# A selective-scan layer in one block: the scan starts after the first chunk's softplus, the other chunks' softplus moves into the scan's units

## The chip, the cores and the metric

The kernel runs on one core of a Trainium2 chip. Its five engines run at the same time, each with a queue of its own, and wait for one another through semaphores: TensorE (PE, matrix products), VectorE (DVE), ScalarE (ACT, activation functions from tables), GpSimd (POOL) and SyncE (SP, which here only issues DMAs). The metric is the time of one execution on the device in microseconds (us), the median of several runs; lower is better.

## The reference

Eight layers follow one another on a residual stream `x` of 2048 tokens by 128 features. The change touches only the first, a selective state-space layer (Mamba) with a feed-forward layer behind it. Cut to what matters:

```
x  = layer_norm(x)                       # twice: the outer norm, then the layer's own
xz = x @ in_proj_w;  xi, z = split(xz)   # 256 channels each
xc = silu(causal_conv4(xi) + conv_b)
dt, B, C = split(xc @ x_proj_w)          # 8, 16, 16 columns
dt = softplus(dt @ dt_proj_w + dt_proj_b)
A  = -exp(A_log)                         # 256 channels x 16 states
for each token t:                        # a recurrence over all 2048
    h = exp(dt[t] * A) * h + dt[t] * B[t] * xc[t]
    y[t] = sum over the 16 states of h * C[t]
y  = (y + D * xc) * silu(z)
x  = x + y @ out_proj_w
x  = x + gelu(layer_norm(x) @ ffn_w1 + ffn_b1) @ ffn_w2 + ffn_b2
```

## The kernel before

Channels lie on the 128 partitions, in two halves (H = 2), and tokens on the free axis, in C = 4 chunks of 512 columns (CW). The layer is made of two blocks. Between two blocks all engines meet at a barrier.

The first block is the projection. For each chunk TensorE transposes the normalised input (`turn`), multiplies it with convolution taps (`taps`) and with the gate weights (`gate`), computes B, C and the rank-8 part of dt (`b_c_rank`), and from the latter the raw dt (`steps_dt`). ACT evaluates the products: `take_taps` and `take_gate` with Silu, `take_high` copies B and C to bf16. Since B and C are wanted to full precision, they are kept as three bf16 parts: `take_high`, then DVE's `first_rest`, ACT's `take_middle`, DVE's `last_rest`, ACT's `take_low`. The softplus is computed as max(v, 0) + ln(1 + exp(-|v|)): ACT's `take_abs` (L561) writes |v| into `dtx`, DVE's `relu_dt` (L404) writes max(v, 0) into `dt`, ACT then runs Exp over two chunks at a time (`exp_of`, L567) and Ln over chunk 0 and chunks 1 to 3 (`ln_of`, L572). At its end DVE adds the two for chunk 0 (L449) and multiplies with `xc` (L451). DVE's `outer_norm` (L379) makes `xo`, the base of the residual, and POOL's `add_bias` (L321) adds a bias to X.

The second block is the scan. It has U = 64 units, one for each chunk and state, chunk by chunk. In unit u TensorE spreads one row of B over all partitions and one of C (`spread`, L632 and L636), DVE multiplies `dtx` with B (`dBx`, L773), ACT computes the decays exp(dt * A) of both halves into PSUM (L720), DVE runs the recurrence of each half (`tensor_tensor_scan`, L784), ACT copies the last column of an earlier unit's `h` (`keep_state`, L712) and C (`Cs`, L726), POOL multiplies h with C (`hC`, L855), and TensorE adds it up over the states (`y_sum`, L645). Everything is double-buffered by u % 2. At the start of each later chunk DVE finishes the one before: `skip` (L756), `gated` (L761), then TensorE's `project` (L654) and DVE's `residual` (L766), which stands in DVE's queue in the fourth unit ahead of its scans. In units 0 to 11 POOL also adds the two parts of the softplus for chunks 1 to 3 (L845) and multiplies with `xc` (L849). SP's `fill` (L100) writes blank rows to memory for the next layer. Behind the last unit follows the feed-forward layer, in the same block.

Each engine's queue is written out in program order, so an instruction that waits holds up all behind it.

Of the kernel before, what the change touches and what calls it, by code (L numbers as in the profile page):

```python
# [24 lines left out]
U32 = mybir.dt.uint32  # L25
ALU = mybir.AluOpType
# [6 lines left out]
P = 128  # L33
# [151 lines left out]
def mamba(k):  # L185
# [22 lines left out]
    with tmp:  # L208
# [47 lines left out]
        s_dtm, s_abs, s_rel, s_exp, s_ln, s_A, s_dt, s_dtx, s_xb = (  # L256
            k.sem("m_" + n) for n in ("dt_mm", "dt_abs", "dt_relu", "dt_exp", "dt_ln", "A", "dt", "dtx", "x_plus_b"))
        col = lambda n: t[n].rearrange("(p o) -> p o", o=1)
        blocks = lambda n: t[n].rearrange("(h p) -> p h", p=P)

        with nc.Block() as block:
            @block.sync
            def _(sp):
                def x_chunk(c):
                    sp.dma_start(k.X[:, tiles_of(c), :],
                                 t["x"][c * CW:(c + 1) * CW, :].rearrange("(t p) d -> p t d", p=P)).then_inc(x_in[c], 16)

                with nc.allow_non_contiguous_dma(reason="small weights"):
                    x_chunk(0)
                    sp.dma_start(cwr[:], t["conv_wT"].rearrange("(o k) d -> o (k d)", o=1)).then_inc(w_in, 16)  # L270
                    sp.dma_start(inw[:], t["in_proj_w"]).then_inc(w_in, 16)
                    sp.dma_start(g1[:], col("ln1_g")).then_inc(w_in, 16)
                    sp.dma_start(b1[:], col("ln1_b")).then_inc(w_in, 16)
                    for c in range(1, C):
                        x_chunk(c)
                    for dst, src in ((cb[:], blocks("conv_b")), (xpw[:], t["x_proj_w"].rearrange("(h p) k -> p h k", p=P)),
                                     (dtw[:], t["dt_proj_w"]), (dtb[:], blocks("dt_proj_b")),
                                     (A[:], t["A_log"].rearrange("(h p) n -> p h n", p=P)),
                                     (w2b[:], t["ffn_b2"].partition_broadcast(P))):
                        sp.dma_start(dst, src).then_inc(w_xp, 16)  # L280
                    for dst, src in ((Dp[:], blocks("D")), (outw[:], t["out_proj_w"].rearrange("(h p) d -> p h d", p=P)),
                                     (g2[:], col("ln2_g")), (b2[:], col("ln2_b")), (w1[:], t["ffn_w1"]),
                                     (w1b[:], t["ffn_b1"].rearrange("(f p) -> p f", p=P)),
                                     (w2[:], t["ffn_w2"].rearrange("(f p) d -> p f d", p=P))):
                        sp.dma_start(dst, src).then_inc(w_out, 16)
                sp.wait_ge(w_out, 16 * 7)

            @block.gpsimd
            def _(pool):
                g = nc.gpsimd  # L290
                exact = dict(allow_small_or_imprecise_dtypes=True)
                g.memset(k.ident[:], 0.0)
                g.memset(k.ones[:], 1.0)
                g.memset(k.mhalf[:], -0.5).then_inc(c_zero, 1)
                pool.wait_ge(c_zero, 1)
                g.affine_select(out=k.ident[:], in_=k.ident[:], compare_op=ALU.not_equal, fill=1.0, base=0,
                                pattern=[[-1, P]], channel_multiplier=1).then_inc(c_id, 1)
                for n, part in enumerate((slice(0, CT), slice(CT, T))):
                    pool.wait_ge(s_ve, n + 1)
                    g.tensor_tensor(both[:, part], both[:, part], k.mhalf[:, part], ALU.pow).then_inc(s_rs, 1)  # L300
                g.memset(xp4[:], 0.0).then_inc(m_z, 1)
                pool.wait_ge(w_xp, 16 * 6)
                pool.wait_ge(m_z, 1)
                g.tensor_copy(xp4[:, :, 0, 0:R], xpw[:, :, 0:R])
                for part in range(1, 4):
                    last = g.tensor_copy(xp4[:, :, part, :], xpw[:, :, R:R + BC])
                last.then_inc(m_xp, 1)
                pool.wait_ge(s_ve, 3)
                g.tensor_tensor(k.rstd[:], k.veps[:], k.mhalf[:, 0:T], ALU.pow).then_inc(s_rs, 1)
                g.memset(sel[:], 0.0).then_inc(m_z, 1)  # L310
                pool.wait_ge(m_z, 2)

                def select(part):
                    g.affine_select(out=sel[:], in_=sel[:], compare_op=ALU.not_equal, fill=1.0, base=-32 * part,
                                    pattern=[[-1, BC], [0, P]], channel_multiplier=1).then_inc(m_sel, 1)
                    pool.wait_ge(m_sel, part)

                def add_bias(c):
                    pool.wait_ge(s_xo, c + 1)
                    xt = k.X[:, tiles_of(c), :]  # L320
                    g.tensor_tensor(xt, xt, w2b[:, None, :].to_broadcast([P, CT, P]), ALU.add).then_inc(s_xb, 1)  # L321

                select(1)
                select(2)
                select(3)
                g.memset(state[:], 0.0)
                g.memset(k.blank[:], 0.0)
                g.memset(k.onesb[:], 1.0)
                g.memset(k.tri[:], 1.0).then_inc(c_more, 1)
                add_bias(0)  # L330
                g.iota(k.each[:], pattern=[[1, k.E]], base=0, channel_multiplier=0, **exact)
                g.iota(k.first_row[:], pattern=[[k.REGION, k.E]], base=0, channel_multiplier=0, **exact)
                g.iota(k.step[:], pattern=[[1, k.step.shape[1]]], base=0, channel_multiplier=0, **exact)
                g.iota(k.token[:], pattern=[[k.N, 2], [P, T]], base=0, channel_multiplier=1)
                pool.wait_ge(c_more, 1)
                g.affine_select(out=k.tri[:], in_=k.tri[:], compare_op=ALU.is_gt, fill=0.0, base=0, pattern=[[1, P]],
                                channel_multiplier=-1)
                g.iota(k.blank[:, :, P].bitcast(U32), pattern=[[P, 2 * k.E]], base=2 * k.N, channel_multiplier=1)\
                    .then_inc(k.made_blank, 1)
                add_bias(1)  # L340
                add_bias(2)
                add_bias(3)

            @block.vector
            def _(dve):
                v = nc.vector

                def stats(c):
                    dve.wait_ge(x_in[c], 16)
                    for i in range(c * CT, (c + 1) * CT):  # L350
                        last = v.bn_stats(k.stats[:, i, :], k.X[:, i, :])
                    last.then_inc(s_st, 1)
                    dve.wait_ge(s_st, c + 1)
                    for i in range(c * CT, (c + 1) * CT):
                        last = v.bn_aggr(k.meanvar[:, i, :], k.stats[:, i, :])
# [2346 lines left out]
```

## Time and profile before

| | |
|---|---|
| median of 3 runs | 1608.6 us (1608.26 to 1610.08) |
| the profiled execution's own time | 1608.58 us |
| its span, first to last instruction | 1606.5 us |
| mean granted TensorE clock | 0.871 |
| busy share of the span | PE 75%, DVE 55%, ACT 40%, POOL 33% |
| the first layer | about the first 368 us |
| end of TensorE's projection work, first dBx | 64.4 us, 80.34 us |

Times of a timeline are from the span's start. Idle time of an engine is printed with what ended it. The granted clock is a share of 2.4 GHz. A row that reads "x2" holds two instructions back to back, which overlap a little.

### The profile page before, as it was taken

The numbers are of one execution on the slowest core, as the hardware profiler recorded it, in microseconds if no ns is written. First come the engines' busy times: TensorE is split into PE (matmuls) and PEld (weight loads), VectorE is DVE, ScalarE is ACT, GpSimd is POOL, SyncE is SP. The second block draws the span as 40 slices with busy tenths as digits, with TensorE's granted clock in tenths as the row PEclk, the third lists the DMA queues.
The fourth block names the chain that finished last, engine by engine and source line by source line (L and its number), as shares of the span: only waits on it lengthen the run. The fifth ranks groups of instructions, "written<-read, shape, count | busy, mean of one in ns | idle before, by whom it ended". The sixth has DMA issues, their size and how long they took to land. (4 is left out here: it accounts for less than half of the span.)

```text
span 1606.5 us, 23917 instructions
## 1 busy us (share of the span) xinstructions
PE 1209.1 (75%) x8263; PEld 726.7 (45%) x8271; DVE 878.5 (55%) x2054; ACT 649.7 (40%) x1106; POOL 531.0 (33%) x661
## 2 busy tenths in 40 slices
PE   8676766784389665089944999969954899969997
PEld 3222222244267444056622777734322676744544
DVE  3498999965244444133346888853662666741110
ACT  2664545541012101033313777637633666632221
POOL 6086656521723210712235222120026444200000
PEclk9789999996589865589975999979975999979999
DMA  2099400004121204111120000010000000020000
GB/s 53 0 197 188 67 1 1 0 1 159 52 54 52 78 6 157 52 44 42 34 79 1 2 2 2 2 41 1 1 9 0 2 2 2 2 75 0 0 0 27
DMA packets 87883, 59.76 MB, mean 37 GB/s; under 512 B 15331, under 2 KB 78709, under 8 KB 87638
## 3 DMA queue, kind: packets, MB, share of 16 engines
q1 hardware_dynamic: 83222, 48.86, 14.2%
q0 software_dynamic: 4544, 9.38, 1.8%
q8 instruction: 69, 1.13, 0.3%
q14 instruction: 48, 0.39, 0.1%
HBM read 29.69 MB, written 28.52 MB: 36 GB/s over the span
## 5 line engine op out<-in xcount | busy, mean ns | idle before, releaser
L855 POOL TENSOR_TENSOR hC<-h,Cs 128x1024 f32<-128x1024 f32 x64 | 153.2, 2394 | 86.8 <-DVE h L784 85.2
L645 PE MATMUL bank<-hC,ident 128*128 128x512 f32 x256 | 135.4, 654 | 41.3 <-POOL hC L855 41.3
L784 DVE TENSOR_TENSOR_SCAN h<-bank,state,dBx 128x512 f32<-128x512 f32 x128 | 157.3, 1271 | 2.2 <-ACT bank L720 0.2
L1157 POOL DMA_INDIRECT moe_answers<-moe_yw,moe_xg x78 | 74.7, 958 | 174.7 <-DVE moe_yw L1254 174.7
L2103 DVE TENSOR_REDUCE window_mx<-bank 128x2 f32<-128x384 f32 x128 | 69.6, 556 | 75.8 <-PE bank L1958 74.8
L1221 ACT ACTIVATE moe_hT<-bank 128x512 f32<-128x512 f32 x78 | 46.6, 597 | 155.5 <-PE bank L1184 155.5
L2103 DVE TENSOR_REDUCE decay_mx<-bank 128x2 f32<-128x512 f32 x128 | 85.2, 686 | 23.8 <-PE bank L1958 23.5
L720 ACT ACTIVATE bank<-dt,A 128x512 f32<-128x512 f32 x128 | 83.2, 682 | 36.5 <-DVE h L784 36.4
L2073 ACT ACTIVATE decay_pb<-bank 128x512 f32<-128x512 f32 x128 | 75.6, 597 | 47.8 <-PE bank L1971 45.1
L645 PEld LDWEIGHTS bank<-hC,ident 128*128 128x128 f32 x256 | 46.4, 200 | 106.1 <-POOL hC L855 68.2
L1193 PE MATMUL bank<-moe_wd,moe_hT 128*128 x624 | 84.5, 280 | 1.9 <-DVE moe_yw L1254 1.9
L178 ACT ACTIVATE xnT<-bank 128x512 f32<-128x512 f32 x24 | 14.3, 597 | 176.6 <-PE bank L169 176.6
L1167 PE MATMUL bank<-ident,moe_xg 128*128 128x128 f32 x78 | 22.5, 289 | 83.1 <-DMA moe_xg<-moe_slots 75.0
L1174 PE MATMUL bank<-moe_wa,moe_xgT 128*128 x156 | 83.4, 617 | 0.0
L967 POOL DMA_INDIRECT moe_slots<-moe_rows,moe_slot x64 | 61.6, 963 | 59.8 <-DVE moe_slot L1060 40.9
L158 POOL TENSOR_TENSOR rstd<-veps,mhalf 128x4 f32<-128x4 f32 (+1 forms) x14 | 23.3, 1662 | 171.3 <-DVE veps L140 171.1
L1193 PEld LDWEIGHTS bank<-moe_wd,moe_hT 128*128 128x128 f32 x624 | 77.5, 196 | 2.6 <-issue 2.6
L2073 ACT ACTIVATE window_pb<-bank 128x384 f32<-128x384 f32 x128 | 61.5, 486 | 40.1 <-PE bank L1971 39.8
L773 DVE TENSOR_TENSOR dBx<-dtx,bank 128x1024 f32<-128x1024 f32 x64 | 76.6, 1197 | 0.9 <-remote 0.9
L726 ACT ACTIVATE Cs<-bank 128x512 f32<-128x512 f32 x64 | 38.2, 596 | 78.9 <-POOL hC L855 58.1
L169 PE MATMUL bank<-ident,xn 128*128 128x128 f32 x64 | 17.2, 424 | 68.5 <-DVE xn L149 68.4
L2604 DVE TENSOR_TENSOR f_ys<-bank,f_s 128x512 f32<-128x512 f32 x4 | 2.8, 692 | 119.4 <-PE bank L2563 119.4
(455 smaller groups left out, 2933.4 us busy)
## 6 DMA issues: line engine op xcount, KB each, us to landing
moe_slots<-blank SPq DMA_DIRECT2D x16, 1040.0 KB, 17.9
moe_xg<-moe_slots SPq DMA_DIRECT2D x78, 65.0 KB, 1.8
moe_wa<-in_moe_w SPq DMA_DIRECT2D x2, 2048.0 KB
moe_back<-moe_answers SPq DMA_DIRECT2D x16, 256.0 KB, 4.7
moe_ba<-in_moe_b SPq DMA_DIRECT2D x1, 2048.0 KB
moe_wu<-in_moe_wu SPq DMA_DIRECT2D x1, 2048.0 KB
deep_w<-in_deep_w SPq DMA_DIRECT2D x3, 512.0 KB, 5.1
moe_answers<-moe_yw,moe_xg POOLq DMA_INDIRECT x78, 2.2
```

What stands on the lines that cost most here:

```text
L645: last = nc.tensor.matmul(sum_bank(hh)[:], k.ident[:], hC[:, u % 2, hh, :], start=(n == 0), stop=(n == NS - 1))
L720: nc.scalar.activation(decay_bank(u, hh)[:], dt[:, hh, cols(c)], ACT.Exp, scale=A[:, hh, n:n + 1]).then_inc(q_dA, 1)
L773: v.tensor_tensor(dBx[:, u % 2], dtx[:, :, cols(c)], b_bank[:, None, :].to_broadcast([P, H, CW]), ALU.mult).then_inc(q_dBx, 1)
L784: v.tensor_tensor_scan(h[:, u % 2, hh, :], decay_bank(u, hh)[:], dBx[:, u % 2, hh, :], state[:, n, hh:hh + 1], ALU.mult, ALU.add).then_inc ...
L855: g.tensor_tensor(hC[:, u % 2], h[:, u % 2], Cs[:, u % 2, None, :].to_broadcast([P, H, CW]), ALU.mult).then_inc(q_hC, 1)
L967: nc.gpsimd.indirect_dma_start(slots, bass.IndirectOffsetOnAxis(index, 0), rows[j][:, i, :], None)\
L1157: nc.gpsimd.indirect_dma_start(answers, bass.IndirectOffsetOnAxis(index, 0), yw[:, i % NY, :], None)\
L1174: nc.tensor.matmul(bank[1 + i % 2][:], xgT[:, i % 2, :], flat(wa), start=True, stop=True).then_inc(s_g, 1)
L1193: last = nc.tensor.matmul(bank[6][:, 0:P], hT[:, i % 2, f, :], wd[:, one, f, :].rearrange("p o d -> p (o d)"), start=(f == 0), stop=(f == ...
L1221: nc.scalar.activation(hT[:, i % 2].rearrange("p f q -> p (f q)"), bank[5 + 2 * (i % 2)][:], ACT.Copy if gated else ACT.Relu).then_inc(s_h ...
L2073: nc.scalar.activation(pb[:, w % 4, :], bank[2 + w % 2][:, 0:2 * HW], ACT.Exp).then_inc(s_ex, 1)
L2103: nc.vector.tensor_reduce(mx[:, 2 * g:2 * g + 2], bank[g % 2][:, 0:2 * HW].rearrange("p (j q) -> p j q", j=2), AX.X, ALU.max, negate=True) ...
```

## The change

Both blocks' queues go into one block, so no barrier stands between them; each engine runs its projection queue and then its scan queue. In detail:

- `take_abs` and `relu_dt` go. ACT's `take_rates` copies the raw dt from PSUM to `dt` with the bias (Identity, two per chunk). `size_of` (Abs), `positive_of` (Relu), `exp_of` and `ln_of` then work on one chunk of 1024 columns each from SBUF.
- ACT loads one named table set for Exp and Ln ahead of them. Before the scan it runs `exp_of` and `ln_of` for chunk 0 only, then `take_high`(2), `take_low`(1), `take_high`(3), `take_rates`(2), `take_rates`(3).
- Chunk 0's sum is one DVE instruction, max(dt, 0) + dtx; chunks 1 to 3 get their Relu on ACT.
- ACT's scan units 1 to 12 hold the other chunks' Abs, Relu, Exp and Ln, one each; units 13, 14 `take_middle`(2), (3) and units 18, 19 `take_low`(2), (3). DVE's units 15, 16 hold `last_rest`(2), (3).
- POOL's sums and products for chunks 1 to 3 stand in units 5 to 16; the outer norm of chunks 2 and 3 moves from DVE to POOL, units 18 and 22, with `add_bias` in units 20 and 24.
- SP issues the fill at once, without a barrier before it.

```
 project_scalar, end
+            for hh in range(H):
+                act.wait_ge(s_dtm, H * c + hh + 1)
+                nc.scalar.activation(dt[:, hh, cols(c)], dt_bank(c, hh)[:], ACT.Identity, bias=dtb[:, hh:hh + 1])\
+                    .then_inc(s_raw, 1)
...
+            nc.scalar.preload_act_table_set("natural_log_exp_and_others")
+            nc.scalar.activation(A[:], A[:], ACT.Exp).then_inc(s_A, 1)
+            exp_of(0)
+            ln_of(0)
+            take_high(last_c - 1)
+            take_low(last_c - 2)
+            take_high(last_c)
+            take_rates(last_c - 1)
+            take_rates(last_c)
 project_vector, end
             take_rank(last_c)
             first_rest(last_c - 1)
             first_rest(last_c)
-            relu_dt(last_c - 1)
-            last_rest(last_c - 1)
-            relu_dt(last_c)
-            last_rest(last_c)
-            outer_norm(last_c - 1)
-            outer_norm(last_c)
...
+            first = dt[:, :, cols(0)]
+            v.scalar_tensor_tensor(out=first, in0=first, scalar=0.0, in1=dtx[:, :, cols(0)], op0=ALU.max, op1=ALU.add)\
+                .then_inc(s_dt, 1)
 scan_scalar, in unit u behind the decays and keep_state, ahead of Cs
+                if u in (1, 5, 9):
+                    size_of(1 + u // 4)
+                if u in (2, 6, 10):
+                    positive_of(1 + u // 4)
+                if u in (3, 7, 11):
+                    exp_of(1 + u // 4)
+                if u in (4, 8, 12):
+                    ln_of(u // 4)
+                if u in (13, 14):
+                    take_middle(u - 11)
+                if u in (18, 19):
+                    take_low(u - 16)
 scan_vector, in unit u behind dBx
+                if u in (15, 16):
+                    last_rest(u - 13)
 scan_gpsimd, in unit u behind hC
-                c = 1 + u // (2 * H)
+                c, n = 1 + (u - 5) // 4, (u - 5) % 4
...
+                if u in (18, 22):
+                    outer_norm(2 + (u - 18) // 4)
+                if u in (20, 24):
+                    add_bias(2 + (u - 20) // 4)
 scan_gpsimd, new
+            def outer_norm(c):
+                for n in range(c * CT, (c + 1) * CT):
+                    last = g.tensor_scalar(xo[:, n, :], k.X[:, n, :], k.meanvar[:, n, 0:1], k.rstd[:, n:n + 1],
+                                           ALU.subtract, ALU.mult)
+                last.then_inc(s_xo, 1)
 scan_tensor, spread(u)
+                if n == 0:
+                    pe.wait_ge(s_lo, c + 1)
+                if u == 0:
+                    pe.wait_ge(m_sel, 3)
+                    pe.wait_ge(s_raw, H * last_c)
+                    pe.wait_ge(s_tev, C)
 scan_scalar, unit 0
+                if u == 0:
+                    act.wait_ge(s_A, 2)
+                    act.wait_ge(s_dt, 1)
+                    act.wait_ge(s_raw, H * C)
```

## Rows read from the trace of the kernel before

**Rows 1.** Stretches: window: length, busy by engine (count), granted clock, DMA share, GB/s.
```profile
40.00:64.40 24.40, 24.40 (x57) 9.64 (x56) 9.43 (x16) 14.14 (x20) 1.41 (x3) 0.98 0.00 1
64.40:80.10 15.70, 0.01 (x1) 0.14 (x2) 10.61 (x17) 13.58 (x16) 2.56 (x2) 0.50 0.00 0
...
90.00:141.00 51.00, 36.86 (x87) 11.53 (x87) 50.51 (x44) 28.41 (x57) 46.70 (x26) 0.99 1.26 193
```

**Rows 2.** Timeline of ACT, 54 to 84: start, busy, line, operation, [idle before].
```profile
56.02 1.33 ACT L561 ACTIVATE dtx<-bank,dtb 128x512 f32<-128x512 f32 x2
...
61.07 0.60 ACT L548 ACTIVATE BC<-bank 128x512 bf16<-128x512 f32 x1 [1.12 <-DVE lr L386]
61.68 1.28 ACT L567 ACT_TABLE_LOAD   x1
62.98 1.91 ACT L567 ACTIVATE dtx<-dtx 128x2048 f32<-128x2048 f32 x1
```

**Rows 3.** Timeline of DVE, 54 to 86.
```profile
71.90 0.69 DVE L398 TENSOR_TENSOR rt<-rt,BC 32x512 f32<-32x512 f32 x1
...
76.12 2.02 DVE L449 TENSOR_TENSOR dt<-dt,dtx 128x1024 f32<-128x1024 f32 x1 [0.32 <-ACT dtx L572]
78.17 1.23 DVE L451 TENSOR_TENSOR dtx<-dt,xc 128x1024 f32<-128x1024 f32 x1
80.34 1.22 DVE L773 TENSOR_TENSOR dBx<-dtx,bank 128x1024 f32<-128x1024 f32 x1 [0.95 <-remote]
81.77 2.46 DVE L784 TENSOR_TENSOR_SCAN h<-bank,state,dBx 128x512 f32<-128x512 f32 x2 [0.21 <-ACT bank L720]
```

**Rows 4.** Timeline of DVE in the steady scan, 92 to 104.
```profile
98.57 1.20 DVE L773 TENSOR_TENSOR dBx<-dtx,bank 128x1024 f32<-128x1024 f32 x1
99.80 2.46 DVE L784 TENSOR_TENSOR_SCAN h<-bank,state,dBx 128x512 f32<-128x512 f32 x2
102.17 1.20 DVE L773 TENSOR_TENSOR dBx<-dtx,bank 128x1024 f32<-128x1024 f32 x1
```

**Rows 5.** Timeline of ACT in the steady scan, 92 to 104.
```profile
95.08 1.30 ACT L720 ACTIVATE bank<-dt,A 128x512 f32<-128x512 f32 x2 [0.52 <-DVE h L784]
...
97.58 0.60 ACT L726 ACTIVATE Cs<-bank 128x512 f32<-128x512 f32 x1 [1.06 <-POOL hC L855]
```

**Rows 6.** Timeline of POOL, 72 to 104 and 140 to 164.
```profile
75.79 1.27 POOL L321 TENSOR_TENSOR X<-X,m_w2b 128x512 f32<-128x512 f32 x1 [0.68 <-DVE xo L379]
...
95.13 2.36 POOL L855 TENSOR_TENSOR hC<-h,Cs 128x1024 f32<-128x1024 f32 x1
...
146.79 3.25 POOL L855 TENSOR_TENSOR hC<-h,Cs 128x1024 f32<-128x1024 f32 x1 [2.44 <-DVE h L784]
...
159.61 2.35 POOL L855 TENSOR_TENSOR hC<-h,Cs 128x1024 f32<-128x1024 f32 x1 [5.73 <-DVE h L784]
```

**Rows 7.** Timeline of TensorE, 54 to 104.
```profile
60.19 4.23 PE L506 MATMUL bank<-lr,dtw 8*128 8x512 f32 x8
...
86.72 3.78 PE L645 MATMUL bank<-hC,ident 128*128 128x512 f32 x4 [0.29 <-POOL hC L855]
...
97.54 1.99 PE L645 MATMUL bank<-hC,ident 128*128 128x512 f32 x4 [0.72 <-POOL hC L855]
```

**Rows 8.** Groups of ACT by line and shape, 40 to 80: count | busy us, mean ns.
```profile
L572 ACT ACTIVATE dtx<-dtx 128x1024 f32<-128x1024 f32 x1 | 1.1, 1057 | 0.0
```

**Rows 9.** Timeline of DVE at the first chunk boundary, 141 to 160.
```profile
142.94 1.40 DVE L756 SCALAR_TENSOR_TENSOR yT<-xc,Dp,bank 128x512 f32<-128x512 f32 x2
144.26 2.45 DVE L784 TENSOR_TENSOR_SCAN h<-bank,state,dBx 128x512 f32<-128x512 f32 x2
...
156.47 0.69 DVE L766 TENSOR_TENSOR xo<-bank,xo 128x512 f32<-128x512 f32 x1 [3.91 <-PE bank L654]
```

**Rows 10.** Groups of POOL by line and shape, whole span: a pow, and a subtract.
```profile
L309 POOL TENSOR_TENSOR rstd<-veps,mhalf 128x16 f32<-128x16 f32 x1 | 3.0, 2954 | 0.0
...
L2269 POOL TENSOR_TENSOR window_left<-window_left,window_qp 128x128 f32<-128x128 f32 x16 | 6.8, 427 | 2.9 <-POOL window_kp L2263 2.9
```

More of the change, by code:

```diff
@@ L620, in mamba, with last_rest, take_middle, take_low @@
         b_bank, c_bank = bank[6], bank[7]
+        def last_rest(c):
+            nc.vector.wait_ge(s_mid, c + 1)
+            wait(nc.vector, s_lo, c - 1)
+            nc.vector.tensor_tensor(rt2[96:128, c % 2, :], rt1[96:128, c % 2, :], BC3[96:128, cols(c)], ALU.subtract)\
+                .then_inc(s_r2, 1)
+        def take_middle(c):
+            nc.scalar.wait_ge(s_r1, c + 1)
+            nc.scalar.activation(BC3[64:128, cols(c)], rt1[64:128, c % 2, :], ACT.Copy).then_inc(s_mid, 1)
+        def take_low(c):
+            nc.scalar.wait_ge(s_r2, c + 1)
+            nc.scalar.activation(BC3[96:128, cols(c)], rt2[96:128, c % 2, :], ACT.Copy).then_inc(s_lo, 1)
@@ new lines, in size_of, with positive_of, exp_of @@
+        def size_of(c):
+            nc.scalar.wait_ge(s_raw, H * (c + 1))
+            nc.scalar.activation(dtx[:, :, cols(c)], dt[:, :, cols(c)], ACT.Abs).then_inc(s_abs, 1)
+        def positive_of(c):
+            nc.scalar.wait_ge(s_abs, c + 1)
+            nc.scalar.activation(dt[:, :, cols(c)], dt[:, :, cols(c)], ACT.Relu).then_inc(s_pos, 1)
+        def exp_of(c):
+            nc.scalar.wait_ge(s_abs, c + 1)
+            nc.scalar.activation(dtx[:, :, cols(c)], dtx[:, :, cols(c)], ACT.Exp, scale=-1.0).then_inc(s_exp, 1)
@@ L658, in turn @@
-                def turn(c):
-                    pe.wait_ge(f_xn, c + 1)
-                    if c == 0:
-                        pe.wait_ge(q_dBx, U)
-                    wait(pe, f_tev, c)
-                    for i in range(CT):
-                        last = nc.tensor.transpose(b_bank[:, i * P:(i + 1) * P], k.xn[:, c % 2, i, :], k.ident[:])
-                    last.then_inc(f_tr, 1)
-                def hidden(c):
-                    pe.wait_ge(f_tev, c + 1)
-                    if c == 0:
-                        pe.wait_ge(q_h, H * U)
-                    for f in range(FB):
-                        wait(pe, f_ev, (c - 1) * FB + f + 1)
-                        nc.tensor.matmul(bank[f][:], w1[:, f * P:(f + 1) * P], k.xnT[:, cols(c)], start=True, stop=True)\
-                            .then_inc(f_h, 1)
@@ L687, in _ @@
-                spread(0)
-                for u in range(U):
-                    c, n = divmod(u, NS)
-                    if u + 1 < U:
-                        spread(u + 1)
-                    if u:
-                        y_sum(u - 1)
-                    if n == 2 and c:
-                        project(c - 1)
-                y_sum(U - 1)
-                turn(0)
-                hidden(0)
-                turn(1)
-                project(C - 1)
-                for c in range(C):
-                    if c + 1 < C:
-                        hidden(c + 1)
-                    if c + 2 < C:
-                        turn(c + 2)
-                    down(c)
+                project_tensor(pe)
@@ L708, in _ @@
+                scan_tensor(pe)
             @block.scalar
             def _(act):
[L710 to L726 removed]
@@ L869, in top_two @@
+                project_scalar(act)
+                scan_scalar(act)
 def top_two(k, dve, act_sem, src, top, ti, tf, s):
```

987 lines of the change are left out of this document (505 added, 482 removed).

## Prediction

> **What bounds the kernel now.** I began with the page. Its chain of work that ended last holds only the last part of the program and says nothing about this change. So I read the part by stretches, then the timeline of each engine around the end of the projection, and last the steady scan.
>
> The stretches [rows 1] split the part in two. From 40 to 64.4 us TensorE is busy all the time (24.40 us). From 64.4 to 80.1 it does 0.01 us of work, while ACT works 13.58 and DVE 10.61 of 15.70. From 90 us on DVE is the full engine (50.51 of 51.00). So the projection is bound by TensorE and the scan by DVE, and between them lie 15.7 us for the softplus of all chunks and what surrounds it. ACT's rows [rows 2] show the first of three table loads there, before Exp; Ln and the scan's Exp load again. DVE's rows [rows 3] end with dt and dtx of chunk 0; the first scan unit starts at 80.34, behind a barrier.
>
> In the steady scan a unit takes 3.60 us, dBx at 98.57 to dBx at 102.17 [rows 4]: dBx and two scans, end to end. ACT has two gaps in each unit, 1.06 us before Cs (waiting for POOL's hC) and 0.52 before the decays, which end at 96.38 for a scan that starts at 99.80, 3.4 us later [rows 4, 5]. POOL's hC takes 2.36, so it idles 1.25 of each 3.60, except where a piece of later chunks' dt or dtx (a two-input 128x512 like add_bias, 1.27) fills it [rows 6].
>
> **The change, part by part: where the first unit starts.** TensorE's order is unchanged up to steps_dt(3), and it sets the pace up to there: those matmuls end at 60.19 + 4.23 = 64.42 [rows 7]. The added size_of(0), 1.06 us by the 1024-column row [rows 8], falls where ACT is busy 14.14 of 24.40 [rows 1] and waits for b_c_rank(1): free; without that cover it would cost its 1.06.
>
> ACT after 56.02: take_rates(1) takes the place of Abs on the same banks, 1.33, to 57.35. Table load 1.30, to 58.65; exp of A some 0.2, to 58.87; exp_of(0) 1.06, to 59.93; ln_of(0) 1.06, to 61.0. I take 1.06 for both from the row of just that size; half of the 2048-column 1.91, 0.96, is the lower bound. Then take_high(2) 0.60 to 61.6, take_low(1) to 62.2, take_high(3) to 62.8, and four Identities at 0.65 (half of Abs's 1.33) to 65.4; the last needs TensorE's 64.42, already past.
>
> DVE waits for take_high(2) with first_rest(2), 61.65 to 62.35 at the 0.69 of its sister last_rest [rows 3], and for take_high(3) with first_rest(3), 62.85 to 63.55. A's negation adds 0.1. Then chunk 0's dt, one instruction: before, it took 2.02 us, beside POOL's add_bias (75.79 to 77.06), while the multiply of the same size behind it, mostly with POOL idle, took 1.23 [rows 3, 6]. Now POOL is idle in both: 1.23 to 64.9, and 1.23 to 66.15. So the scan doesn't follow the softplus quite at once: DVE's sum stands 2.6 us behind Ln, queued behind the two first_rests, and these behind ACT's copies. The first spread waits for PE (64.42) and for take_rates(2) (64.1) and is done by 65.2. dBx(0) thus starts near 66.15 against 80.34, **14.2 us** earlier. Its scan had waited 0.21 more for the decays [rows 3]; now these run from 65.4 to 66.7 and dBx ends at 67.4: 14.4 in all. Bounds: 13.6 if dt takes 2.02, 14.6 with 0.96 for Exp and Ln.
>
> A rule of the Trainium skill may be weighed here. In the trace the load starts 0.01 us after the copy before it ends, and Exp starts 1.30 after the load does [rows 2]. The Trainium skill (ScalarE: Activation LUTs, "What ACT_TABLE_LOAD costs") adds some 1.38 us of drain to each switch. By that the sum would be 13.0 in place of 14.4; the rows have no room for it and decide.
>
> **What the scan takes in.** ACT: twelve 1024-column activations (Abs, Relu, Exp, Ln for three chunks), one in each of units 1 to 12, at 1.06. Each stands behind keep_state, where ACT waits 1.06 anyway [rows 5]. If one takes 0.5 more, the gap before the decays takes it, and behind that lie the 3.4. Price 0; with no cover 12.7 us in all. The four copies in units 13, 14, 18 and 19 are shorter and fit likewise.
>
> DVE: the relu_dt and the outer norms that go lay in waits or in the gap, which is already counted as gone. New on the bound engine are last_rest(2) and (3), in units 15 and 16. What an insert between dBx and the scans costs there the first boundary shows: two skips, 1.40 busy, start at 142.94 and the scan at 144.26, 0.66 each [rows 9]. Two last_rests of 0.69: **1.3 us**. Lower bound 1.0, upper 1.4.
>
> POOL: the dt and dtx pieces move from units 0-11 to 5-16 at the same price; hC and a piece make 3.6, the unit itself. Their input is ready a unit ahead (ln_of(1) is in ACT's unit 4, POOL's first piece in its unit 5). outer_norm on POOL is eight tensor_scalars of 128x128, which no row shows. The nearest are its two-input 128x128 ones, 427 ns [rows 10]: four make 1.7. In unit 18 POOL idles 5.73 [rows 6]. In unit 22, 1.7 exceeds the 1.25 by 0.45, but hC has 2.3 us in hand (it ends at 97.49, the scan that needs it starts at 99.80): hidden. add_bias, 1.27, fits the idle time. Lower bound 0; upper: at 1.1 each a group of four exceeds 1.25 + 2.3 by 0.9, so 1 us.
> hC took 3.25 beside DVE's gated product, not 2.36 [rows 6]. A last_rest, also with two SBUF inputs, would stretch it by about 0.5, inside the 2.3. The Trainium skill (GPSIMD Engine Reference, "1. Specifications") says that GpSimd's SBUF interface contends with just such DVE instructions; by that too the sum stays, but it is the rule that speaks against putting them here.
>
> SP: the fill starts when the blank is written, near 40 us. The scans of [rows 4] ran at 2.46 with a DMA share of 1.26 [rows 1], and nobody waits for the fill before the next part: 0. A barrier goes; it is in the 14.2.
>
> **Sum.** 14.4 - 1.3 = 13.1 us off. The profiled execution took 1608.58 with a span of 1606.5 and the median is 1608.6, so both give **1595.5** (span 1593.4).
>
> **Rivals.**
> (a) Half the clock. TensorE idled from 64.4 to 80.1, and its first y_sum took 3.78 us, later ones 1.99 [rows 7]: the granted clock was 0.50, 1.2 GHz, then 0.99 [rows 1]. At 1.2 GHz TensorE's share of a unit is about 4.8, over DVE's 3.6. DVE lost nothing to it then. Now TensorE idles only some 3 us, from 68.2 to dBx(1)'s end at 71.3, so I expect no worse. But each slow unit past the 2.3 in hand costs 1.2, and at the chunk boundary DVE waited 3.91 us for project [rows 9], which another level of the clock moves by up to 1.8 (half a y_sum), three times. Price +1 to +5: 1596.5 to 1600.5.
> (b) Tables not saved: if Exp and Ln still load by turns, a 1.28 load stands before ln_of(0) and delays all behind it, and six more stand in units 4 to 13. Four of ACT's units then hold 4 x (2.09 + 1.06) + 2.56 = 15.2 us against DVE's 14.4: 0.8 of backlog a group, 2.4 in three, inside the 3.4. Price 1.3: 1596.8. The kernel before reloads at each turn. The Trainium skill (ScalarE: Activation LUTs, "Table sets: the hidden batching unit") names a set that holds both, which would exclude this.
> (c) More: the boundaries meet the full clock and give up to 1.5 each: 1591 to 1594.
> (d) The other side: POOL's tensor_scalar is far slower than its tensor_tensor, as its pow is (2.95 us for 16 columns [rows 10]). Slack for the eight is about 5.7 + 1.3 + 2 x 2.3 = 11.6. From (11.6 + 13.1)/8 = 3.1 us each the gain is gone; at pow's pace, some 20 us each, the kernel ends near 1595.5 + 160 - 11.6 = 1744. Against: 427 ns for subtract.
> (e) The gap only moves: the scan starts early and waits within, say for chunk 1's d_dt at unit 16. POOL's last piece for it is in unit 8, eight units ahead.
>
> **How the numbers follow.** Forecast 0.60 (own range 1594.0 to 1596.5), (a) 0.20, (b) 0.08, (c) 0.07, (d) 0.02, (e) 0.03. The time predicted is the forecast's. The range takes in (b), nearly all of (a) and the milder part of (c), also because later parts, shifted by 13 us, can meet the clock otherwise: 1591.5 to 1600.0. 0.2%, about what a measurement of this kernel can tell from no change, is 3.2 us; only (d) and (e) miss it: faster 0.95, same 0.03, slower 0.02.
>
> **What would show it.** Right: one table load near 57.4 us and no other until Gelu; first dBx near 66.2; a pitch of 3.6 in units 2 to 14 and 4.3 in 15 and 16; the part ends 13 us sooner. Wrong: DVE idle in units 1 to 25 and released by ACT's decays or POOL's hC; POOL's outer norm over 1 us an instruction; y_sum at 3.78 for several units on end; a first dBx after 68 us.

## The result, and the profile after

The changed kernel takes 1598.06 us (median of 6 runs, 1596.48 to 1601.84) against 1610.55 for the kernel before beside it (6 runs, 1608.26 to 1614.39): a ratio of 0.9922 with a 95% interval of 0.9904 to 0.9940. That is 12.5 us off. It is faster by 0.8% and inside the predicted range; the forecast itself, 1595.5, is 2.6 too low and its own range, to 1596.5, ends 1.6 too low. Most of that is the base: the forecast took 13.1 off 1608.6, and beside the changed kernel the one before took 1.95 more. Taken as a gain, 13.1 was forecast and 12.5 came. The profiled execution took 1598.1 with a span of 1596.3, so the span is only 10.2 shorter than before. The same file was timed again later: 1597.85 (6 runs), ratio 0.9918 [0.9901, 0.9935], and in that trace the span is 8.3 shorter. A single pair of traces thus tells the size of the whole gain to 2 us or so; its parts inside the first layer can be read to 0.1.

ACT's timeline of the changed kernel, 50 to 90 us, answers to [rows 2]:

```profile
56.63 1.32 ACT L571 ACTIVATE dt<-bank,dtb 128x512 f32<-128x512 f32 x2
57.97 1.28 ACT L596 ACT_TABLE_LOAD   x1
59.26 0.23 ACT L597 ACTIVATE A<-A 128x32 f32<-128x32 f32 x1
59.40 1.04 ACT L300 ACTIVATE dtx<-dtx 128x1024 f32<-128x1024 f32 x1
60.47 1.06 ACT L304 ACTIVATE dtx<-dtx 128x1024 f32<-128x1024 f32 x1
61.44 0.58 ACT L566 ACTIVATE BC<-bank 128x512 bf16<-128x512 f32 x1
62.69 0.60 ACT L566 ACTIVATE BC<-bank 128x512 bf16<-128x512 f32 x1
63.31 2.42 ACT L571 ACTIVATE dt<-bank,dtb 128x512 f32<-128x512 f32 x4
```

Exp (L300) and Ln (L304) run back to back on one load. DVE's timeline of the same stretch answers to [rows 3]:

```profile
62.05 0.69 DVE L430 TENSOR_TENSOR rt<-bank,BC 64x512 f32<-64x512 f32 x1 [0.47 <-ACT BC L566]
63.32 0.69 DVE L430 TENSOR_TENSOR rt<-bank,BC 64x512 f32<-64x512 f32 x1 [0.58 <-ACT BC L566]
64.14 1.22 DVE L468 SCALAR_TENSOR_TENSOR dt<-dt,dtx 128x1024 f32<-128x1024 f32 x1
65.39 1.23 DVE L471 TENSOR_TENSOR dtx<-dt,xc 128x1024 f32<-128x1024 f32 x1
66.71 1.22 DVE L787 TENSOR_TENSOR dBx<-dtx,bank 128x1024 f32<-128x1024 f32 x1
67.97 2.46 DVE L802 TENSOR_TENSOR_SCAN h<-bank,state,dBx 128x512 f32<-128x512 f32 x2
```

The first dBx starts at 66.71, 13.6 us ahead of before. The two windows of the changed kernel, the projection and the scan up to 130 us, answer to [rows 1]:

```profile
40.00:65.00 25.00, 24.48 (x58) 9.90 (x58) 7.87 (x16) 18.15 (x27) 1.83 (x4) 0.99 1.17 187
66.60:130.00 63.40, 43.69 (x95) 13.92 (x97) 62.66 (x53) 47.59 (x83) 51.63 (x27) 0.90 1.27 192
```

DVE is busy for 62.66 of 63.40 us from the first unit on: no wait took the place of the barrier. But "busy" hides one thing. DVE's timeline at units 15 and 16:

```profile
120.80 1.20 DVE L787 TENSOR_TENSOR dBx<-dtx,bank 128x1024 f32<-128x1024 f32 x1
122.03 1.84 DVE L279 TENSOR_TENSOR rt<-rt,BC 32x512 f32<-32x512 f32 x1
123.90 2.46 DVE L802 TENSOR_TENSOR_SCAN h<-bank,state,dBx 128x512 f32<-128x512 f32 x2
126.28 1.20 DVE L787 TENSOR_TENSOR dBx<-dtx,bank 128x1024 f32<-128x1024 f32 x1
127.50 1.83 DVE L279 TENSOR_TENSOR rt<-rt,BC 32x512 f32<-32x512 f32 x1
```

last_rest takes 1.84 here and took 0.69 in [rows 3]: the same instruction with the same shape. POOL's timeline, with the two stretches of interest (units 15 to 17, and the end of unit 18 to unit 25; they answer to [rows 6]):

```profile
120.97 2.35 POOL L886 TENSOR_TENSOR hC<-h,Cs 128x1024 f32<-128x1024 f32 x1
123.28 1.71 POOL L865 TENSOR_TENSOR dt<-dt,dtx 128x512 f32<-128x512 f32 x1
...
143.79 3.14 POOL L873 TENSOR_SCALAR xo<-X,meanvar,rstd 128x128 f32<-128x128 f32 x4
...
161.52 3.13 POOL L873 TENSOR_SCALAR xo<-X,meanvar,rstd 128x128 f32<-128x128 f32 x4
164.61 4.66 POOL L886 TENSOR_TENSOR hC<-h,Cs 128x1024 f32<-128x1024 f32 x2
```

hC (120.97 to 123.32) had begun before last_rest came (122.03), and kept its 2.35. A group of four outer norms takes 3.13, or 785 ns each. TensorE's timeline behind the second group:

```profile
161.60 1.98 PE L635 MATMUL bank<-hC,ident 128*128 128x512 f32 x4 [0.72 <-POOL hC L886]
164.11 0.38 PE L623 MATMUL bank<-BC,sel 128*128 128x512 bf16 x1 [0.53 <-DVE dBx L787]
167.01 3.56 PE L635 MATMUL bank<-hC,ident 128*128 128x512 f32 x4 [2.52 <-POOL hC L886]
170.41 0.38 PE L619 MATMUL bank<-BC,sel 128*128 128x512 bf16 x1
```

TensorE waits 2.52 for the late hC and then runs y_sum in 3.56 in place of 1.98, so the next B row comes late.

Since every unit starts with one dBx, the starts of the 64 dBx make a ledger. All are from DVE's timelines of the two traces. A length is counted to the dBx that follows and named by it: "unit 16" is the distance from dBx 15 to dBx 16, so an insert in the code of unit 15 lengthens unit 16.

```
unit   before    after    ahead   what happened in between
 0      80.34    66.71    13.63
15     134.62   120.80    13.82   no wait for the decays (0.2); 3.60 a unit else
17     141.83   131.74    10.09   two last_rests: units of 5.48 and 5.46
20     159.45   148.22    11.23   first residual: 8.08 before, 6.94 after
26     181.08   170.83    10.25   after POOL's second outer norm: 3.60 before, 4.59 after
36     222.45   212.81     9.64   second residual: 6.59, 7.18
52     286.04   274.71    11.33   third residual: 7.18, 5.50
63     325.69   314.36    11.33
```

From there to the end 1.1 us of the 11.3 is given back, behind the scan, where the code is the same.

### The profile page after: what moved, and what is told of

Read it like the earlier page. It is cut to its first block and busy times, and to the rows that moved or that the text cites. A ratio compares the mean times of both kernels' runs of the same rounds, so it can differ in the third digit from the quotient of the medians.

```text
span 1596.3 us, 23923 instructions
## 1 busy us (share of the span) xinstructions
PE 1209.1 (76%) x8263; PEld 727.3 (46%) x8271; DVE 870.9 (55%) x2038; ACT 653.9 (41%) x1115; POOL 538.0 (34%) x669
```

## The experiments

Each kernel below differs from the changed kernel by the diff shown, unless it says otherwise. Units are counted as in the ledger. A single run can't tell a gain of 2 us from none by its time; what such a run shows is read from its trace.

### What last_rest costs, and why

The two suspects: last_rest is slow because POOL is at work on the same SBUF, or because of DMA traffic (192 GB/s in this window). And which POOL instruction is it? First, last_rest is only moved behind the scans of its unit.

```diff
@@ scan_vector, unit u
-                if u in (15, 16):
-                    last_rest(u - 13)
                 ... the two scans ...
+                if u in (15, 16):
+                    last_rest(u - 13)
```

> last_rest(2) and (3) stand behind the scans of units 15 and 16 instead of between dBx and the scans. Theory (held by hC): a DVE instruction with two SBUF inputs that comes while POOL's hC runs is held until hC ends; behind the scans it starts before hC, as gated does. Then last_rest takes 0.69 us instead of 1.84, the units of 5.48 and 5.46 become about 4.3, hC beside it grows from 2.35 to about 2.9, and the scan is 2.3 to 2.5 us shorter: time 0.9985 of the changed kernel. Rival (the traffic of the fill or the partial partitions make it 1.84 wherever it stands in this stretch): last_rest stays near 1.84 and nothing changes.

Measured: 1595.94 us (1595.08 to 1601.07), ratio to before 0.9910 [0.9879, 0.9941]. Units 16 and 17 take 4.44 and 4.46, not 5.48 and 5.46: 2.04 us less, where 2.3 to 2.5 were expected. By time alone this isn't told from the changed kernel, 0.9922 [0.9904, 0.9940]. DVE and POOL at unit 15, each from its own timeline of this kernel:

```profile
124.62 0.69 DVE L279 TENSOR_TENSOR rt<-rt,BC 32x512 f32<-32x512 f32 x1
```
```profile
124.67 2.85 POOL L886 TENSOR_TENSOR hC<-h,Cs 128x1024 f32<-128x1024 f32 x1
```

Now last_rest starts 0.05 ahead of hC, runs at 0.69, and it is hC that grows, by 0.50. So the order of arrival decides who pays. What is left, 0.84 and 0.86 a unit, is its 0.69 and some 0.15 of overlap, since dBx used to start 0.1 before the scans' end (in the changed kernel the scans run from 118.43 for 2.46, to 120.89, and dBx starts at 120.80).

Second, last_rest is moved to where neither POOL's dt piece nor the fill's traffic is beside it.

```diff
@@ scan_vector            @@ scan_scalar
-  if u in (15, 16):      -  if u in (18, 19):
-      last_rest(u - 13)  -      take_low(u - 16)
+  if u in (27, 28):      +  if u in (29, 30):
+      last_rest(u - 25)  +      take_low(u - 27)
```

> last_rest(2) and (3) keep their place between dBx and the scans, but in units 27 and 28 (take_low in 29 and 30), where POOL has no dt or dtx piece and the fill has ended. Theory (held by hC): hC runs there too, so last_rest still takes about 1.8 us and each unit 5.4 to 5.5. Rival 1 (POOL's piece is what collides): 0.69 us and units of about 4.2. Rival 2 (the fill's traffic): also 0.69 us.

Measured: one run, 1600.37 us, span 1598.6. Units 16 and 17 are back at 3.60 and 3.61, units 28 and 29 take 5.47 each, and last_rest 1838 ns on average: the price went along unchanged. DVE and POOL at unit 28, each from its own timeline:

```profile
172.22 1.84 DVE L279 TENSOR_TENSOR rt<-rt,BC 32x512 f32<-32x512 f32 x1
```
```profile
171.16 2.35 POOL L886 TENSOR_TENSOR hC<-h,Cs 128x1024 f32<-128x1024 f32 x1 [1.51 <-DVE h L802]
```

POOL has no piece there, and from 167 to 180 us the DMA share is 0.00. Neither the piece nor the traffic holds last_rest; what both places share is hC, and the place behind dBx, which the third kernel tests.

Third, the price by kind of operand. This kernel also has last_rest behind the scans, as above, and the split norm from below, so that nothing else is in the way, and it adds one scratch instruction a unit ahead of the scans (extra work; the output doesn't depend on it):

```diff
+                if u in range(27, 32):     # one input, SBUF
+                    v.tensor_scalar(rt2[96:128, 0, :], left, 1.0, None, ALU.mult)
+                if u in range(38, 48):     # two inputs, both SBUF
+                    v.tensor_tensor(rt2[96:128, 0, :], left, high, ALU.subtract)
+                if u in range(54, 64):     # two inputs, one of them PSUM
+                    dve.wait_ge(q_dA, H * u + 1)
+                    v.tensor_tensor(rt2[96:128, 0, :], decay_bank(u, 0)[96:128, :], high, ALU.subtract)
```

> The price of an insert between dBx and the scans, by its operands, each writing a scratch tile of 32x512: on e1's and e6's placement, a tensor_scalar with one SBUF input in units 27 to 31, a tensor_tensor with two SBUF inputs in units 38 to 47, a tensor_tensor with one input in PSUM and one in SBUF in units 54 to 63. Theory (an instruction that uses both of DVE's SBUF read ways is held while POOL's hC runs): the two-input ones lengthen each unit by 1.87 us, the one with PSUM by about 0.6; the single-input one, if it also uses both ways, by about 1.6, else 0.6. Rival (any insert at this place waits 1.2 us, say for dBx to drain): all three cost about 1.8.

Measured: one run, 1630.47 us. The units take 5.18 (+1.58), 5.45 (+1.85) and 4.31 (+0.71), to 0.01 in every unit of each group. Three rows of DVE's timeline, and of POOL's the hC beside the first:

```profile
172.48 1.57 DVE L800 TENSOR_SCALAR rt<-rt 32x512 f32<-32x512 f32 x1
...
265.01 1.84 DVE L802 TENSOR_TENSOR rt<-rt,BC 32x512 f32<-32x512 f32 x1
...
321.56 0.70 DVE L805 TENSOR_TENSOR rt<-bank,BC 32x512 f32<-32x512 f32 x1
```
```profile
171.41 2.35 POOL L897 TENSOR_TENSOR hC<-h,Cs 128x1024 f32<-128x1024 f32 x1 [0.99 <-DVE h L810]
```

The instruction with a PSUM input costs its own 0.70 and no more, so the place behind dBx costs nothing by itself; the same with both inputs in SBUF costs 1.84. So it is the SBUF reads beside hC. Both kinds that are held end just behind hC: the tensor_scalar at 174.05, 0.29 after hC's 173.76, and last_rest in the changed kernel at 123.87, 0.55 after hC's 123.32. The fp32 tensor_scalar, with only one input, is held as well: it can't be told here whether it reads by the same way or is held for another reason. The Trainium skill (GPSIMD Engine Reference, "1. Specifications") names DVE instructions with two SBUF inputs, and those in a two-port mode, as the ones that contend with GpSimd. The prices of the two tensor_tensors agree with that; that the tensor_scalar ran in such a mode is shown by no run here. Who waits, and how long, that section doesn't say; the runs do: the later one.

### POOL's outer norm

The stall at unit 26 is put down to 3.13 us of norm in one piece. Two ways out: keep these norms on DVE ahead of the scan, or spread them over more units.

```diff
@@ project_vector, ahead of A's negation   @@ project_gpsimd, end
+            outer_norm(last_c - 1)        +            add_bias(2)
+            outer_norm(last_c)            +            add_bias(3)
@@ scan_gpsimd: both calls of outer_norm and of add_bias go
```

> The outer norm of chunks 2 and 3 is on DVE ahead of the scan again, and add_bias on POOL there. Theory: the eight tensor_scalars (3.08 us before) push the first dBx to about 69.5 us, while the scan gets back only the 1.0 us that unit 26 lost behind POOL's late hC; net 1.5 to 2.5 us slower than the changed kernel. Rival (POOL's norm costs the scan more than it shows): no slower than the changed kernel.

Measured: 1603.37 us, ratio to before 0.9951 [0.9934, 0.9968], span 1602.4. Unit 26 is at 3.60 again, but the first dBx starts at 70.70, 4.0 later than in the changed kernel and later than the 69.5 expected. At the last unit 3.7 are lost and in the medians 5.3, where the expectation had 1.5 to 2.5. DVE's timeline shows the two terms:

```profile
64.10 3.09 DVE L419 TENSOR_SCALAR xo<-X,meanvar,rstd 128x128 f32<-128x128 f32 x8
...
68.44 2.17 DVE L475 TENSOR_TENSOR dtx<-dt,xc 128x1024 f32<-128x1024 f32 x1
```

The norms cost 3.09, and chunk 0's product took 2.17 in place of 1.23. add_bias (67.26 to 69.52 on POOL) had begun before it, which is the same holding once more. So moving the norm off DVE is worth about 4 us at the start for 1.0 in unit 26.

```diff
-                if u in (18, 22):
-                    outer_norm(2 + (u - 18) // 4)
-                if u in (20, 24):
-                    add_bias(2 + (u - 20) // 4)
+                if u in (18, 20, 22, 24):    # two of the four tensor_scalars each
+                    outer_norm(2 + (u - 18) // 4, (u - 18) // 2 % 2)
+                if u in (26, 28):
+                    add_bias(2 + (u - 26) // 2)
```

> POOL's outer norm is split in halves of two tensor_scalars over units 18, 20, 22 and 24, add_bias in 26 and 28. Theory (3.13 us at once in unit 22 made hC late, TensorE idled 2.52 us, its clock fell and y_sum took 3.56): a half of 1.57 us exceeds POOL's 1.25 of idle time by 0.3 only, hC is never over 0.4 late, y_sum stays at 1.98 and unit 26 comes back from 4.59 to 3.60. Rival (the loss at unit 26 is a fall of the clock that comes anyway): a unit near 26 still takes over 4 us.

Measured: one run, 1596.3 us, span 1594.5. Two tensor_scalars take 1.57 to 1.59, and unit 26 is at 3.60, as expected. The 1.0 comes of the four in one piece, then, and not of POOL doing them. But the piece alone isn't enough for it. The kernel with the residual moved, below, has the four in one piece as well; its TensorE waits the same 2.52 us behind them, and there the timeline goes on like this:

```profile
163.71 2.41 PE L635 MATMUL bank<-hC,ident 128*128 128x512 f32 x4 [2.52 <-POOL hC L886]
...
166.76 2.77 PE L635 MATMUL bank<-hC,ident 128*128 128x512 f32 x4
```

With y_sum at 2.41 in place of 3.56 (and 2.77 for the one behind it), the B row comes in time, unit 26 takes 3.64 and nothing is lost. In the seven other traces with the norm in one piece in unit 22, y_sum takes 3.56 to 3.68 and unit 26 4.59 to 4.70. The granted clock was 0.55 from 167.0 to 170.6 in the changed kernel, and 0.80 from 163.7 to 166.1 in this one. So the price needs both, the late hC and a low clock right behind the wait; the first can be removed.

### Is it the block, the table set, or the softplus in the units?

Three parts of the change alone. First all of the softplus, both last_rests and the norms ahead of the scan, but in one block and with one table set:

```diff
@@ project_scalar, end
-            exp_of(0)
-            ln_of(0)
             ... take_high, take_low, take_rates ...
+            for c in range(1, C):
+                size_of(c)
+                positive_of(c)
+            ... take_middle(2), (3) ...
+            for c in range(C):
+                exp_of(c)
+            ... take_low(2), (3) ...
+            for c in range(C):
+                ln_of(c)
@@ scan_scalar, scan_vector, scan_gpsimd: all inserts in the units go
```

> One block and one table set as in the change, but all the softplus, the middle and low copies, both last_rests and the outer norms stand ahead of the scan, as before. Theory (the gain is the work moved into the units, the merging only saves the barrier and table loads): first dBx at 77 to 80 us, scan pitch 3.60 throughout, the kernel 0 to 3 us faster than before. Rival (merging itself brings the gain): first dBx before 72 us and the kernel over 8 us faster than before.

Measured: 1609.88 us (10 runs), ratio to before 0.9995 [0.9975, 1.0015]. The first dBx starts at 81.98, later than before's 80.34 and later than expected: Abs and Relu now are six 1024-column operations of ACT's own, and Exp and Ln of four chunks take 3.90 each behind them. So with all the softplus ahead, one block and one table set give nothing: what they save (priced one by one below) the added Abs and Relu take again. The gain is in what the scan's units take over.

Second the change with its barrier kept between the two parts:

```diff
@@ the block
                 project_vector(dve)
-                scan_vector(dve)
                 ... and so for each engine ...
+        with nc.Block() as block:
+            ... scan_sync, scan_gpsimd, scan_vector, scan_tensor, scan_scalar ...
```

> The change with its order of work, but a barrier between projection and scan again. Theory (order, not merging): the barrier costs 0.7 to 1.3 us, first dBx near 67.6 us, and all else of the gain stays, 10 to 12 us faster than before. Rival (without the merged block the early start is lost): first dBx after 72 us.

Measured: 1599.94 us, ratio to before 0.9923 [0.9898, 0.9948]. The first dBx:

```profile
67.55 1.22 DVE L787 TENSOR_TENSOR dBx<-dtx,bank 128x1024 f32<-128x1024 f32 x1 [1.33 <-PE bank L619]
```

It waits 1.33 for the first B row, which TensorE may spread only behind the barrier, and starts 0.84 later than in the changed kernel. But the projection itself ran 0.40 earlier in this trace: take_rates(1) starts at 56.23, not at 56.63. From there to the first dBx it is 11.32 in place of 10.08, so the barrier costs 1.24, inside the expected 0.7 to 1.3. The medians don't show it apart from the changed kernel. The title of the change names the one block first, but that is a small part of it.

Third the change without the named table set:

```diff
-            nc.scalar.preload_act_table_set("natural_log_exp_and_others")
```

> Without the preload of the set that holds both Exp and Ln. Theory (b of the prediction): eight table loads of 1.28 us from 58 us to unit 13 in place of one; first dBx 1.3 to 1.5 us later than in the changed kernel (66.7), units 2 to 14 still at 3.60 since ACT's backlog is under the 3.4 us in hand. Rival (ACT becomes the bound of these units): units over 3.8 us around 4, 8 and 12.

Measured: one run, 1598.43 us, span 1596.6. Before Ln, and once more in each turn between the decays and the inserts, ACT now loads a table; three of the eight added loads in its timeline:

```profile
60.36 1.28 ACT L304 ACT_TABLE_LOAD   x1
...
80.44 1.28 ACT L304 ACT_TABLE_LOAD   x1
83.30 1.28 ACT L718 ACT_TABLE_LOAD   x1
```

The first dBx starts at 67.89, 1.18 later, and 1.28 later counted from take_rates(1), which starts 0.10 earlier here (56.53). All units up to the 15th keep their 3.60. One load is on the path and costs its length; the other seven lie in ACT's slack. In neither kernel does a load show a second pause: Ln starts 1.30 behind the start of its load (61.66), and the first dBx is later by the 1.28 of the load and no more.

### The two waits that are left

Two things still hold DVE up in the changed kernel. The table of waits of the changed kernel, DVE, 64 to 317 us (total, times, longest):

```profile
DVE xo L777 <- PE bank L646: 7.1, 3, 3.0
DVE dBx L787 <- PE bank L619: 0.9, 1, 0.9
```

Before it was 9.3 in three waits at the same place. There `residual` stands ahead of the fourth unit's scans and waits for project, which is queued behind y_sums whose length depends on TensorE's clock. The edit lets it stand behind them.

```diff
-                if c and n == 3:
-                    residual(c - 1)
                 ... the two scans ...
+                if c and n == 3:
+                    residual(c - 1)
```

> The changed kernel, with residual(c) behind the scans of the fourth unit of a chunk instead of ahead of them, so that project and a slow y_sum run beside the scans. Theory (the 5.50 to 8.08 us of that unit are DVE waiting for TensorE, the spread being its granted clock): the unit comes to 4.2 to 4.4 us in all three chunks, 6 to 7 us less than the changed kernel's 6.94 + 7.18 + 5.50. Rival (DVE waits elsewhere for the same TensorE work, at dBx of the next unit): the sum of units 19 to 21 of each chunk falls by under 1 us.

Measured: one run, 1595.3 us, span 1593.5. Units 20, 36 and 52 take 4.19, 4.40 and 4.71 (6.94, 7.18, 5.50 in the changed kernel); so the three are 6.3 us shorter; the third is above the expected 4.2 to 4.4. dBx of unit 61 starts at 299.36 against 307.15, 7.8 ahead: the 6.3, a first dBx 0.6 earlier, and 0.9 in unit 26, of which below. The span of the whole program is only 2.8 shorter in this trace; the other 5 are lost behind the scan, where the code is the same, and no run shows why.

And the start of the scan: DVE's sum for chunk 0 waits behind two first_rests that the scan doesn't need yet.

```diff
-            first_rest(last_c - 1)
-            first_rest(last_c)
             ... A's negation, the sum of chunk 0 ...
+            first_rest(last_c - 1)
+            first_rest(last_c)
             ... the product of chunk 0 ...
```

> DVE adds chunk 0's two parts ahead of first_rest(2) and (3), which then stand between the sum and the multiply. Theory (the sum waits only for its place in the queue): sum at about 61.6 us, first dBx at about 65.7 us instead of 66.7, then bound by take_rates(2) and the first spread; the first scan at 67.0 instead of 68.0. Rival (ACT's decays behind take_rates(3) are the limit): first dBx earlier but the first scan not before 67.8.

Measured: one run, 1598.44 us, span 1596.7. From DVE's timeline of this kernel:

```profile
61.45 1.22 DVE L466 SCALAR_TENSOR_TENSOR dt<-dt,dtx 128x1024 f32<-128x1024 f32 x1
...
65.35 1.22 DVE L787 TENSOR_TENSOR dBx<-dtx,bank 128x1024 f32<-128x1024 f32 x1
```

The scan starts 1.36 earlier. Of that, 0.25 is a projection that ran earlier (take_rates(1) at 56.38), and 1.11 the exchange, where some 1.0 was expected. The time doesn't show it. The three boundaries take 7.28, 7.19 and 5.51, 0.34 more at the first, and unit 26 0.11 more, so 0.9 of the 1.36 is left at the last unit, and that is lost behind the scan. Against the second trace of the changed kernel (first boundary 5.51, below) even the last unit is 0.5 later. One run can't tell what the exchange is worth in the whole program.

### All of them together, and the change once more

The last_rest, norm, residual and first_rest edits in one kernel, and the changed kernel on the same chip beside it:

> e1, e6, e8 and e10 together. From the ledger of the changed kernel: 1.4 us from the earlier sum, 2.0 from last_rest behind the scans, 1.0 from the split norm, 6.5 from residual: 10.9 off the changed kernel, first scan unit at 65.4, end of unit 63 near 303.5. Time 0.985 to 0.987 of the kernel before. If the gains overlap (a rival), over 0.988.

> The changed kernel itself again, beside the others on the same chip: 0.991 to 0.994 of the kernel before, first dBx at 66.2 to 67.0, units 16 and 17 at 5.4 to 5.5, unit 26 at 4.6; the unit with residual anywhere from 5.5 to 8.1.

Measured: 1591.76 us (5 runs, 1586.97 to 1594.02) for the four edits, ratio to before 0.9878 [0.9857, 0.9898], against 1597.85 (0.9918 [0.9901, 0.9935]) for the changed kernel. Its first dBx starts at 65.65, unit 26 takes 3.61, and the boundaries 4.43, 4.72 and 4.83. dBx of unit 63 starts at 304.69, 21.0 ahead of before and 9.7 ahead of the changed kernel, the span is 18.0 and 7.8 ahead. The 9.7 are 1.1 at the start, 2.0 from last_rest, 1.0 from the norm and 5.6 from the boundaries, where 10.9 were expected with 6.5 from the boundaries. In the medians 6.1 of them are seen, and the ratio lies between the expected 0.985 to 0.987 and the 0.988 of its rival. It is the fastest version of the study; the interval of its ratio lies wholly below the other's. The residual no longer waits:

```profile
142.04 0.69 DVE L777 TENSOR_TENSOR xo<-bank,xo 128x512 f32<-128x512 f32 x1
```

The second trace of the unchanged file has units 16, 17 and 26 at 5.47, 5.47 and 4.70, as in the first, but the three boundaries at 5.51, 7.20 and 5.51, where the first had 6.94, 7.18 and 5.50. The costs of last_rest and of the norm repeat; those of the boundaries don't. What decides them is in TensorE's timelines: the last y_sum and the project before the first residual.

```
                          y_sum  project  residual's unit
before                     3.78     2.77     8.08
first_rests behind         3.75     1.96     7.28
changed, first trace       3.42     1.95     6.94
changed, second trace      1.98     1.95     5.51
norm split                 1.99     1.95     5.50
```

The unit is 5.50 plus what y_sum takes over 1.98 and project over 1.95: 5.50 + 1.80 + 0.82 = 8.12 for before, 6.94 for 3.42. The later boundaries follow it, too: 6.60 for the 3.08 and 1.95 of before's second, measured 6.59. TensorE's instructions in the scan are the same in all five, but for when they come. What in their timing sets the clock isn't shown; the same file gave both values. Whether DVE stands waiting for it is in the program's hands.

## Why the prediction was right, and where a size was off

**The start of the scan: right.** Forecast 66.15, measured 66.71, and 66.13 to 66.80 in the six other traces with the same start. The 0.56 comes ahead of all steps: the projection ran 0.6 later in this trace, so that take_rates(1) began at 56.63, not at 56.02 [rows 2]. Over the traces of the changed code it begins at 56.06 to 56.73. Counted from there to the first dBx, the chain takes 10.07 or 10.08 in all seven, against the 10.13 of the forecast and 24.32 before: a gain of 14.24, where 14.2 was forecast. The chain itself came as worked out: table load 1.28, two 1024-column activations at 1.04 and 1.06, two first_rests, then sum and product of 1.22 and 1.23, and the claim that the sum stands behind the two first_rests is borne out by the 1.11 that their exchange gave. The doubt whether the sum takes 2.02 or 1.23 is settled, too: with POOL idle it takes 1.22, and with add_bias begun before it the product took 2.17.

**ACT's, POOL's and SP's shares of the inserts: free, as said.** Units 2 to 15 keep 3.60, with POOL's pieces, twelve 1024-column activations, and the fill's 192 GB/s. Two more pieces grew to 1.71 beside the two last_rests, and nothing waited for them. In the run without the table set ACT's slack took seven more loads.

**last_rest: the term that was mis-sized.** "Two last_rests of 0.69: 1.3 us" measured 3.73 (units of 5.48 and 5.46 for 3.61 and 3.60), outside the upper bound of 1.4. The step that failed is the choice of the nearest row. Two skips between dBx and the scans, 0.66 each [rows 9], read one PSUM input each, and the third price above shows that such an instruction pays nothing for hC. The prediction did see that last_rest has two SBUF inputs, but let hC pay for it (0.5), on the row where gated stretches hC to 3.25. There gated begins first. Behind dBx it is hC that has begun, and DVE waits. This miss of 2.4 is the largest in the sum.

**POOL's outer norm: right place, size outside the estimate.** 785 ns each, not 427. The bound gave a cost of 1 us for 1.1 us an instruction; that cost came at 0.785 already, because the 2.3 of slack counted for hC and not for what hangs on it. TensorE, kept waiting 2.52, ran y_sum in 3.56, and the next B row was late by 0.91. That is the mechanism of rival (a), half the clock, but set off by another term, and it cost 1.0. The rest of rival (a) didn't come: the slow y_sums at the very start (3.75, then 2.22) cost DVE nothing.

**The other rivals.** (b), tables not saved: it didn't happen, and where it was made to happen it cost 1.28, near its 1.3. (d) and (e) are excluded, DVE being busy 62.66 of 63.40 us. (c), luckier boundaries: in this pair of traces they gave 1.14 and 1.68 and took 0.59, 2.2 in all, which hid most of the miss on last_rest. Over all traces with the residual ahead of the scans its unit takes 5.50 to 8.08, and the same file gave 6.94 and 5.51 at its first one. The prediction was right to call it chance; that moving the residual takes most of it out was not in it.

**The sum.** 13.6 + 0.2 - 3.7 - 1.0 + 2.2 = 11.3 at the last unit, where 13.1 was forecast. That the whole came out so near, 12.5 for 13.1, is in part luck: without the 2.2 of the boundaries 9.1 would have been left at the last unit. Behind it 1.1 was lost. The place of the largest loss is known, its cause isn't: from the first write of the routers' logits (the tile moe_lg, 388.9 us before) to their last use (636.1) the trace of before takes 247.2 us, and the thirteen other traces, with the same code there, take 249.5 to 253.2, whether they come to it 21.0 us later than before (the kernel of the three prices) or 21.2 earlier (the four edits together). The changed kernel enters this stretch 11.6 ahead, leaves it 8.7 ahead and ends 10.2 ahead. So it is not the shift that costs; it is as well possible that the one trace of before was quick there. With one trace of before this stays open. It is a part of why the spans differ by 10.2 and the medians by 12.5; the rest is that the profiled execution of before took 1608.58 and the median beside the changed kernel was 1610.55.

## What to carry to other kernels

Between a stage bound by one engine and a stage bound by another, work of a third engine that the second stage needs only later belongs into the second stage's slack. Here the first unit came 14.2 us earlier by the whole change; the merged block gave 1.2 of that and the one table set 1.3, and with all the softplus ahead of the scan nothing was left. When an instruction is put into a full engine's queue, look at what the neighbour on SBUF is doing when it arrives: with both inputs in SBUF, ahead of POOL's long instruction it cost 0.69, and behind its start 1.84. And slack of a buffer's reader is slack for that reader alone; an engine that is kept idle by it may come back at the lower clock and be late for somebody else.

## What the runs showed of the hardware that wasn't expected

- A DVE instruction that reads two SBUF inputs and comes while POOL's 128x1024 product runs takes 1.84 us in place of 0.69, and ends 0.55 after POOL's; an fp32 tensor_scalar from SBUF is held too (a unit 1.58 longer), one with a PSUM input isn't (0.71 longer). If DVE's begins first, POOL's product grows instead, from 2.35 to 2.85, or 3.25 beside a 128x1024 one.
- POOL's 128x128 tensor_scalar with two per-partition operands takes 785 ns, 1.8 times its two-input 128x128 subtraction of 427 [rows 10]; the same on DVE takes 0.39 (8 in 3.09 us).
- After the same wait of 2.5 us TensorE's next y_sum took 3.56 to 3.68 in seven traces and 2.41 in another (the one behind it 2.77), in place of 1.98. The same file gave 3.42 and 1.98 for the y_sum ahead of its first boundary in two traces.
